# First cross attention of a two-layer decoder: four fp32 products become three rounded passes of high and low parts, and GpSimd takes the bias and residual adds

## The reference

```python
Q = x                                   # also X stays as the outer residual
q = layernorm(Q) * ln1_g + ln1_b        # 2048 rows of 256
q = split_heads(q @ wq)                 # 16 heads of 64, 1024 columns
q = q / l2norm(q)                       # each head of each row
k = unit rows of layernorm(ctx) @ wk    # done in the stage ahead
P[b] = blockdiag(k.T @ (ctx @ wv)) @ wo # 1024 x 256 for each of the 4 sequences
Q = Q + q @ P[b] + bo                   # "att" in the kernel
h = gelu((layernorm(Q) * ln2_g + ln2_b) @ w1 + b1)   # 1024 columns, gelu behind b1
X = X + Q + h @ w2 + b2
# then the first mixture of experts: layernorm, a projection, a gate over 8 experts
```

## Time and profile before

| | us |
|---|---|
| three runs | 2818.91, 2825.59, 2827.2 (median 2825.59) |
| span of the profiled execution | 2811.1 |
| keys, from 530.00 to the barrier at 935.88 | 405.9 |
| queries loop, 935.88 to the first hidden block at 1088.14 | 152.3 |
| MLP loop, 1088.14 to the last output tile at about 1229.05 | 140.9 |
| the last sequence's gate, to the next stage at 1249.60 | 20.6 |

### The profile page before, as it was taken

How to read it: one execution, slowest core, us unless ns; L and a number is a source line. 1 busy time by engine, 2 the same in 40 slices (tenths; PEclk the granted TensorE clock), 3 DMA queues, 4 the chain that set the end, 5 groups by cost and what they waited for, 6 DMA issues and landing times.

```text
span 2811.1 us, 31753 instructions
## 1 busy us (share of the span) xinstructions
PE 2409.8 (86%) x10916; PEld 1572.3 (56%) x10916; DVE 2115.2 (75%) x3160; ACT 1499.8 (53%) x2623; POOL 1030.0 (37%) x750
## 2 busy tenths in 40 slices
PE   6989896689998899968995798997778987899998
PEld 2333432467776566747984233333333444799998
DVE  5999999798986465447894899999864653577776
ACT  6676573345665222325884865766313344366773
POOL 3889998200000000010121599988702134100004
PEclk8999998899999799978997899999878887899999
DMA  4032040570000000012331321303085221256553
GB/s 177 2 120 96 26 145 0 192 258 1 24 1 1 36 1 30 8 66 101 133 134 53 121 84 37 121 6 127 0 120 106 53 77 63 87 192 220 209 199 94
DMA packets 101602, 247.29 MB, mean 88 GB/s; under 512 B 9285, under 2 KB 65361, under 8 KB 94274
## 3 DMA queue, kind: packets, MB, share of 16 engines
q1 hardware_dynamic: 88530, 222.43, 24.4%
q0 software_dynamic: 5376, 14.70, 1.5%
q10 hardware_dynamic: 7536, 8.13, 1.2%
HBM read 187.96 MB, written 48.81 MB: 84 GB/s over the span
## 4 chain that ended last, share of the span: by engine, by line
PE 42%; DVE 25%; ACT 11%; issue 9%; POOL 8%; SPq 1%; DMA 1%; ACTq 1%; POOLq 0%; DVEq 0%
DVE psum L756 7%; PE psum L496 5%; PE psum L109 5%; PE psum L111 5%; PE psum L110 5%; POOL bu L370 4%; PE psum L116 3%; POOL ch L413 2%; ACT g L3498 2%; ACT WH L3351 2%; PE psum L1416 2%; DVE ch L773 2%; PE psum L1386 2%; PE psum L1402 2%; DVE ch L756 2%
## 5 line engine op out<-in xcount | busy, mean ns | idle before, releaser
L370 POOL TENSOR_TENSOR bu<-u,row 128x1024 f32<-128x1024 f32 x254 | 595.2, 2357 | 138.6 <-DVE psum L756 50.6
L496 PE MATMUL psum<-ch,ident 128*128 128x512 f32 x1024 | 514.3, 635 | 114.4 <-DVE ch L773 63.4
L756 DVE TENSOR_TENSOR_SCAN psum<-psum,bu 128x1024 f32<-128x1024 f32 x210 | 479.9, 2285 | 21.6 <-ACT psum L588 21.5
L496 PEld LDWEIGHTS psum<-ch,ident 128*128 128x128 f32 x1024 | 190.7, 199 | 402.3 <-issue 183.9
L588 ACT ACTIVATE psum<-dt,A 128x511 f32<-128x511 f32 x512 | 332.1, 681 | 0.4
L773 DVE TENSOR_TENSOR ch<-psum,row 128x1024 f32<-128x1024 f32 x210 | 256.6, 1222 | 5.7
L3498 ACT ACTIVATE g<-psum,bias 128x256 f32<-128x256 f32 x248 | 101.3, 471 | 131.0 <-PE psum L111 126.8
L460 PE MATMUL psum<-hT,inw 128*128 128x512 f32 x256 | 130.5, 639 | 26.1 <-ACT xs L534 18.9
L3320 POOL DMA_INDIRECT R<-m1res,gi x26 | 26.1, 1005 | 337.5 <-DMA m1res<-ob 321.3
L1770 POOL MEMSET ones<- 128x128 f32 x1 | 0.2, 204 | 405.5 <-ACTq L3643 405.5
L109 PE MATMUL psum<-WH,hs 128*128 128x256 f32 x496 | 144.7, 292 | 4.6 <-DVE hs L3578 2.3
(11 more groups left out here) (426 smaller groups left out, 6226.1 us busy)
## 6 DMA issues: line engine op xcount, KB each, us to landing
W<-in_m1W SPq DMA_DIRECT2D x24, 2052.0 KB, 8.6
row<-Ascr SPq DMA_DIRECT2D x64, 512.0 KB, 5.5
row<-Bscr SPq DMA_DIRECT2D x64, 512.0 KB, 5.8
m1buf<-zt SPq DMA_DIRECT2D x8, 2048.0 KB, 16.8
W<-in_m0W SPq DMA_DIRECT2D x16, 1024.0 KB, 5.7
m1res<-ob ACTq DMA_DIRECT2D x23, 256.0 KB
m0buf<-zt SPq DMA_DIRECT2D x2, 2064.0 KB, 18.5
xe<-m0buf SPq DMA_DIRECT2D x8, 516.0 KB, 7.9
```

What stands on the lines that cost most here:

```text
L370: e.tensor_tensor(m.bu[i % 3][:, :, :], u, m.row[:, g, 0, :, :], ALU.mult).then_inc(*m.fed.up)
L496: p = pe.matmul(m.y, k.ident, m.ch[i % RING_C][:, j, :], start=False, stop=g == UNITS - 1 and j == 1)
L756: dve.tensor_tensor_scan(to, flat, m.bu[i % 3][:, :, :].rearrange("p a n -> p (a n)"), 0.0, ALU.mult, ALU.add).then_inc(*m.scan.up)
```

## The change

All four products of the stage (queries, att, hidden, output) call `mm3` where they called one plain fp32 matmul. For that each operand has to exist twice. ACT makes the high parts and DVE the low parts of what is made in the stage: the turned rows (`qT`, now two copies and two subtractions for each sequence, where each engine copied one half), the turned unit tiles (`qh`, both halves by ACT, then both low parts by DVE), and the gelu, which goes into one of three float buffers `ge` (they lie over P of sequence 1), is copied to a high part by ACT and subtracted by DVE (`low(n)`); ACT may start gelu n only when low part n-3 is done. The high parts of P (four), w1 and w2 are made by ACT inside the queries loop, their low parts by POOL, in place. High and low part of wq are made in the stage ahead, in its turn 43 of 52. POOL also takes over `+ bo` (on Q before att is added), `+ b2` and `+ Q` (on X), each for four tiles in one instruction, and starts the gate's constants only when the last query tile's squares are summed, since the gate's tables now lie over `sq`, `kn`.

```diff
             for h in range(2):
                 for j in range(2):
-                    p = pe.matmul(m.kvb[i % 2][:, h, :], m.qT[b % 2][:, j, 128 * t:128 * t + 128], m.wq[:, j, 512 * h:512 * h + 512],
-                                  start=j == 0, stop=j == 1)
+                    p = mm3(pe, m.kvb[i % 2][:, h, :], [w[:, j, 128 * t:128 * t + 128] for w in m.qT[b % 2]],
+                            [w[:, j, 512 * h:512 * h + 512] for w in m.wqs], j == 0, j == 1)
...
             for hp in range(8):
-                p = pe.matmul(bank[:, 0:D], m.qh[n % 2][:, hp, :], m.P[n // 4][:, hp, :], start=hp == 0, stop=hp == 7)
+                p = mm3(pe, bank[:, 0:D], [w[:, hp, :] for w in m.qh[n % 2]], [w[:, hp, :] for w in m.Ps[n // 4]], hp == 0, hp == 7)
...
# keys_act, turn i of 52
+            if i == 3 * ST + 4:
+                act.copy(m.wqs[0], m.wq[:, :, :]).then_inc(*m.wq_hi.up)
# keys_pool, at its end
+    pool.wait_ge(*m.wq_hi(0))
+    pool.tensor_tensor(m.wqs[1], m.wq[:, :, :], m.wqs[0], ALU.subtract).then_inc(*m.wq_lo.up)
...
# queries_dve, turned tile n = i - 1
-            dve.tensor_copy(m.qh[n % 2][:, 0:4, :], bank.rearrange("p (j n) -> p j n", j=4)).then_inc(*m.qh0.up)
+            for h in range(2):
+                bank = own.use()
+                dve.wait_ge(*m.qhh(2 * n + h))
+                dve.tensor_tensor(ql[:, 4 * h:4 * h + 4, :], bank.rearrange("p (j n) -> p j n", j=4), qh[:, 4 * h:4 * h + 4, :], ALU.subtract) \
+                    .then_inc(*m.qhl.up)
...
-            dve.tensor_tensor(m.Q[:, n, :], m.Q[:, n, :], vec["bo"][:, :], ALU.add).then_inc(*m.x2.up)
...
# queries_dve, MLP loop: rows2 is now a generator, and the order is
+        low(8 * b)
+        step(rows)
+        step(rows)
+        low(8 * b + 1)
         if b:
             x_inverse_dve(k, dve, 8 + b - 1)
             gate_rows_dve(k, g, dve, b - 1)
-        for t in range(4 * b, 4 * b + 4):
-            dve.tensor_tensor(k.X[:, t, :], k.X[:, t, :], m.Q[:, t, :], ALU.add).then_inc(*k.v.up)
-            dve.wait_ge(*k.v.last())
-            dve.tensor_tensor(k.X[:, t, :], k.X[:, t, :], vec["b2"][:, :], ALU.add).then_inc(*m.sums.up)
-            if b and t % 4 == 1:
-                gate_turned_dve(k, g, dve, b - 1, bank["f1"])
+        low(8 * b + 2)
+        step(rows)
+        low(8 * b + 3)
+        step(rows)
+        step(rows)
+        low(8 * b + 4)
+        low(8 * b + 5)
+        if b:
+            gate_turned_dve(k, g, dve, b - 1, bank["f1"])
+        low(8 * b + 6)
+        low(8 * b + 7)
...
# queries_act, queries loop, at the end of turn i
+        if i == 0:
+            w_high(0, m.w1s[0], m.w1[:, :, :])
+        if i == 1:
+            P_high(1)
+        if i == 3:
+            w_high(1, m.w2s[0], m.w2[:, :, :])
+        if i in (5, 9):
+            P_high(2 + i // 9)
...
# mlp_pool
+    P_low(0)
+    bo(0)
+    w_low(0, m.w1[:, :, :], m.w1s)
+    P_low(1)
+    bo(1)
+    w_low(1, m.w2[:, :, :], m.w2s)
+    for b in range(B):
+        with_row(k.X, b, "b2", m.b2_in)
+    bo(2)
+    P_low(2)
+    sums(0)
+    bo(3)
+    P_low(3)
+    pool.wait_ge(*m.q_sum(NT - 1))
     gate_consts_pool(k, g, pool)
+    for b in range(1, B):
+        sums(b)
```

More of the change, by code:

```diff
@@ L831, in keys_make, with twins, carved, al @@
     m.ho, m.P_in = c("heads_out", 8 * B), c("P", 8 * B)
+def twins(k, ctx, shape, name):
+    with ExitStack() as own:
+        whole = k.make(shape, name=name, ctx=own)
+    return whole, k.make(shape, F32R, name=name + "l", ctx=ctx)[:, :, :]
+def carved(place):
+    at = [0]
+    def al(shape, name):
+        n = math.prod(shape[1:])
+        o = place[:, at[0]:at[0] + n]
+        at[0] += n
+        return o.rearrange("p (a c) -> p a c", a=shape[1]) if len(shape) == 3 else o
+    return al
 def xattn0_make(k, ctx, inner):
@@ L1331, in keys_pool, with q_cols_pe @@
     pool.memset(m.mT[:, :, :], 0.0).then_inc(*m.mt_zero.up)
-def q_cols_pe(k, m, pe, own, rows_in, src, b, signal, t0, t1):
+    pool.wait_ge(*m.wq_hi(0))
+    pool.tensor_tensor(m.wqs[1], m.wq[:, :, :], m.wqs[0], ALU.subtract).then_inc(*m.wq_lo.up)
+def q_cols_pe(k, m, pe, own, rows_in, src, b, signal, low):
     banks = []
-    for free in (t0, t1):
+    for j in range(2):
         banks.append(own.bank(pe))
-        own.freed_by(free(b))
+        own.freed_by(low(2 * b + j))
     for t in range(4):
@@ L1378, in queries_pe @@
                 p.then_inc(*turned.up)
[L1379 removed]
+                own.freed_by(m.qhl(2 * n + h))
         if i >= 2:
@@ L1530, in out, with low @@
         if t % 4 == 0:
-            dve.wait_ge(*m.sums(t + 3))
+            dve.wait_ge(*m.sums(t // 4))
         dve.tensor_tensor(k.X[:, t, :], k.X[:, t, :], bank[:, 0:D], ALU.add).then_inc(*m.x_out.up)
-    rows2(0)
-    own.use()
-    cols2(0, own.use())
+    def low(n):
+        o = n % 8
+        if n >= 8 and o == 0:
+            dve.wait_ge(*m.mlp(4 * (n // 8) - 1))
+        dve.wait_ge(*m.hh(n))
+        dve.tensor_tensor(m.hT[1][:, o, :], m.ge[n % 3], m.hT[0][:, o, :], ALU.subtract).then_inc(*m.hl.up)
+    for _ in rows2(0):
+        pass
+    cols2(0, own.use(), own.use())
     for b in range(B):
         bank = second_banks(own, b)
+        rows = rows2(b + 1) if b + 1 < B else iter(())
         if b:
@@ L1582, in queries_act, with P_high, w_high @@
     own = BankOrder(m.turns)
+    def P_high(b):
+        if b >= 2:
+            act.wait_ge(*m.att(4 * (b - 2) + 3))
+        act.copy(m.Ps[b][0], m.P[b][:, :, :]).then_inc(*m.P_hi.up)
+    def w_high(i, o, w):
+        act.wait_ge(*m.w_m(1))
+        act.copy(o, w).then_inc(*m.w_hi.up)
     def q_cols(b):
-        bank = own.use()
-        own.use()
         act.wait_ge(*m.qT_at(b))
@@ L1589, in q_cols, with cols2 @@
             act.wait_ge(*m.q_rows(4 * (b - 2) + 3))
-        act.copy(m.qT[b % 2][:, 0, :], bank).then_inc(*m.qT0.up)
-    def cols2(b, bank):
+        for j in range(2):
+            act.copy(m.qT[b % 2][0][:, j, :], own.use()).then_inc(*m.qTh.up)
+    def cols2(b, *banks):
         act.wait_ge(*m.mT_at(b))
@@ L1597, in cols2 @@
             act.wait_ge(*m.q_rows(4 * (b + 2) + 3))
-        act.copy(m.qT[b % 2][:, 0, :], bank).then_inc(*m.mT0.up)
+        for j in range(2):
+            act.copy(m.qT[b % 2][0][:, j, :], banks[j]).then_inc(*m.mTh.up)
+    P_high(0)
     for i in range(NT + 2):
@@ L1741, in gate_make @@
     c = m.count
+    with ExitStack() as own:
+        m.wqh = k.make([128, 2, 1024], F32R, name="wqh", ctx=own)
     m.XF, m.lg = al([128, NT, D + 2], "XF"), al([128, NT, E], "lg")
```

153 lines of the change are left out of this document (94 added, 59 removed).

## The result

The changed kernel takes 2839.34 us (median of 4 runs, 2838.68 to 2839.64) beside 2824.24 for the kernel before: a ratio of 1.0056, interval 1.0041 to 1.007. It is slower by 15 us, where the prediction had 2825 and no change that can be told. The stage itself can be read much more exactly than the whole. From DVE's first row of the queries (934.93) to the first transfer behind the barrier (1264.27) it takes 329.3 us; before it took 313.7 (935.88 to 1249.59), and 313.8 in a second trace of the kernel before. All of the 15 us lies there, within what executions scatter. The two spans, 2811.1 before and 2837.3 after, differ by 26 us. Some 11 of these lie behind the barrier and belong to the first trace: behind the barrier it has 1561.5 us, the changed kernel 1573.0, and the second trace of the kernel before 1572.4.

The account below looks back on a forecast made before the run. PE was taken to bound both loops. Queries -13.8, MLP -13.1, POOL holding DVE +22.0 and keys +4.0 summed to -0.9 us, giving 2825 us, no change that can be told, range 2802 to 2840.

Parts of the forecast that it names:

- What a product costs: All four products: three rounded passes cost less than plain fp32, 20.6 us a loop, 41 us if PE never waits.
- Queries loop, without POOL: Queries loop up to the first hidden block, leaving out POOL's effect: -13.8 us, of 20.6.
- The walk: Tile by tile reckoning of each engine's order in the queries loop: first hidden block at 1074.3, -13.8 us without POOL.
- What POOL does to DVE: Mostly queries loop: POOL's SBUF instructions hold DVE's `q_rows` and lengths for whole instructions, PE waiting: +22.0 us.
- a weak step: Queries loop: that PE pays in full for each POOL hold of DVE, named among the weakest steps.
- the low parts of the gelu wait behind GpSimd's sums: MLP loop: gelu low parts, with two SBUF inputs, would also wait behind three POOL sums of 2.35 us.
- Keys stage: Stage ahead: POOL's 4.49 us low part of wq holds DVE; bounds 0 and 4.5, chosen +4.0 us.
- MLP loop: MLP loop: cheaper products less PE's waits around the gate give -13.1 us, of 20.6; periods at 33 us.
- The sum: Whole kernel: -13.8 - 13.1 + 22.0 + 4.0 = -0.9 us, rounded to 2825 us.
- B: Rival, faster: POOL holds DVE where PE has slack; a third of 26 us paid gives 2807; chance 0.30.
- C: Rival, slower: ACT's gelu and copy, bound to DVE, pace the MLP loop, which gives nothing back: 2838; chance 0.25.
- the upper end of 2840: Top of the forecast range for the whole kernel, set by rival C; about 1 in 10 left beyond each end.

Follow-up runs that it names:

- the run with GpSimd cut: Changed kernel with GpSimd's nineteen added instructions cut to 8 columns, high parts read for low ones: 2821.93 us, ratio 0.9975 to the kernel before, stretch 157.9.
- the three moves: ACT high parts right behind squares; DVE low parts before clamp; att before columns, P2/P3 copies before statistics root, against changed kernel: 2806.61 us; with GpSimd cut: 2789.03.

## Why the prediction was wrong, step by step

**What a product costs: right.** Three passes of 512 columns take 0.70 us in the rows' products (0.684 predicted), and att's 24 take 2.9 (2.86).

**Queries loop, without POOL: the step that failed.** "The walk gives ... -13.8 us" should have read +5.6. The walk let a turn's banks go as they did before, when ACT and DVE copied half each and the longest wait was 1.6 us. After the change DVE's subtraction is the only thing that frees a bank, it stands behind the unit rows, and at turns 2, 6 and 10 five banks are wanted in a ring of four. The size is shown by the run with GpSimd cut (157.9 instead of 138.5), and that it lies in the order inside a turn by the same kernel with the three moves (138.9). That the banks are the reason rests on the chain of turn 10 and on the waits that went with the moves; the share of ACT's copies of P2 and P3 (1.88 of the 9.8 us of turn 10), which also were moved, was not measured apart. Part of the loss is TensorE's clock, which the prediction had at nothing: 4.0 us with GpSimd's work in place, from the run that fills the waits. Without GpSimd's work the three waits are 14.4 us and the slow atts behind them 5.2 us longer than 2.96 each, together 19.5, close to the 19.0 that the moves took away.

**What POOL does to DVE: right, in size and mechanism.** +22.0 predicted, 21.4 measured in stretch, and DVE's own durations say 22. The places were right as well: `q_rows` of sequences 0, 1 and 2 are held for 4.1, 4.2 and 6.7 us (4.2, 4.45 and 6.2 predicted), the lengths of tiles 2, 4, 6 and 10 for 2.0, 0.8, 2.0 and 2.0 (2.0, 1.2, 1.8 and 1.9). That PE pays nearly in full for each, called a weak step, held too.

The Trainium skill's rule in "SBUF — State Buffer", "Who interferes with whom", that a DVE instruction with two SBUF inputs and a GpSimd instruction that reads SBUF exclude each other for a whole instruction, agrees with these traces: DVE's four steps beside b2 last 1.14, 2.46, 2.56 and 2.44 us. That the low parts of the gelu wait behind GpSimd's sums is not seen: the three sums of sequences 1 to 3 ran from 1096.65 to 1107.8, ahead of the first hidden product at 1114.23, and the 32 low parts took 0.66 to 0.69 us.

**Keys stage: the mechanism right, the price wrong.** GpSimd's low part of wq ran from 843.27 for 5.10 us, and held the first of four TENSOR_SCALAR of DVE for 4.71 us; the four took 5.67 us in all:

```profile
843.82 5.67 DVE L152 TENSOR_SCALAR Q<-X,xmv,xrs 128x256 f32<-128x256 f32 x4
```

The same four take 1.38 us in the kernel before, so DVE lost 4.3. But PE waited 0.79 us there and no more: the term of +4.0 should have been near its lower bound. The start of the queries scatters from 933.8 to 940.8 over all traces, most of it from the stages ahead of keys. From GpSimd's clearing of `mT` at the start of keys to the first `q_rows` it is 406.5 and 408.0 us in the two traces of the kernel before and 408.2 in the changed kernel's, so keys lost between 0.2 and 1.7 us, and two traces of one kernel differ by as much.

**MLP loop: right in size, and in the main in its place.** From the first hidden product to the last output product 124.5 us, before 137.3: -12.8, predicted -13.1. The hidden blocks of sequences 1, 2 and 3 start 32.9 and 33.3 us apart (33 predicted). Moving the copy of the turned gate rows gave 5.2 us of what was left, so the loss was where the prediction had it; but PE's waits ahead of the projection were 1.84, 0.34 and 2.02 us, not 2 to 2.5 each. Behind the loop 1.4 us were lost that the prediction does not have: the last projection takes 6.74 us instead of 5.42, at a granted clock of 0.54 instead of 0.67.

**The sum.** -13.8, -13.1, +22.0 became +5.6, -12.8, +21.4, and +1.4 came behind the loop: 15.6, beside the stage's 329.3 - 313.8 = 15.5. The +4.0 of keys, which is outside that stage, became 0.2 to 1.7. The rivals B and C were both wrong as mechanisms: DVE's long instructions did cost PE their full length, and the MLP loop did give its 13 us. That 2839 still lies under the upper end of 2840 is luck: that end stood for C's 13.1 us, and was met by an error of 19.4 us in the queries loop less some 3 in keys. (The lower end is also off by 2: a fifth of POOL's price gives 2804, not 2802.)

## What to carry to other kernels

When a copy out of PSUM becomes "high part by one engine, then low part by another", the bank is held until the second is done; find where that second instruction stands on its engine, and count the banks of the fullest turn, before pricing the product. Here three moves inside a turn, one of which puts DVE's two subtractions ahead of the clamp, took 21.7 us off the stretch and turned a loss of 15 us (ratio 1.0056) into a small gain (0.9975); which of the three does most was not measured. Work given to an idle GpSimd was not free where DVE reads SBUF beside it: price each GpSimd instruction at what is left of it when DVE meets it, if DVE is on the path (21.4 us of 22 here), and at next to nothing if it is not (4.3 us of DVE in keys, 0.79 of PE). Cutting instructions to a few columns with all semaphores kept is a quick way to measure what they cost their neighbours.

## What was unexpected of the hardware

After waits of PE of 5.2, 6.6 and 7.9 us the att behind stands at a granted clock of 0.59, 0.53 and 0.65 and takes 4.65, 5.07 and 4.27 us instead of 2.9; sixteen useless passes of 3.7 us in the wait made the whole stretch 4.0 us shorter. An instruction of 16 elements for each partition, DVE's clamp, took up to 4.45 us instead of 0.17 beside GpSimd. Cutting GpSimd's low parts into quarters and its adds of bo and b2 into halves shortened the stretch by only 0.4 us: the clamp still stood once for 4.13 us, past the ends of two pieces, so a piece's end does not always let DVE in.
